# The last chunk of rows finds its 153rd largest value by halving thresholds on ScalarE instead of by repeated MAX8 on VectorE

## The chip, the cores and the metric

One NeuronCore of a Trainium2 chip runs the whole program in one launch. The metric is the device time of an execution in microseconds (us), so lower is better. The kernel before takes 1554.31 us, the median of three runs (1549.61 to 1554.51).

## The reference, cut to what matters

Four residual layers, each followed by a layer norm, over x of 64 x 128 x 512 floats. The change touches layers 0 and 2, which choose neighbours (N = 512 nodes, k = 153):

```python
x_norm = xn / max(norm(xn, axis=-1), 1e-12)
mean_sim = einsum('nbl,mbl->nm', x_norm, x_norm) / B       # 512 x 512
_, idx = top_k(mean_sim, k + 1)                            # per row
# of these the node itself is dropped and the first k = 153 others are kept
mask = zeros((N, N), bool).at[rows, idx].set(keep)
A = where(mask, mean_sim, 0);  deg = A.sum(axis=0)
dinv = where(deg > 0, rsqrt(deg), 0)
An = dinv[:, None] * A * dinv[None, :]
out = einsum('sd,sbl->dbl', An, einsum('nbl,lo->nbo', xn, adj)) + bias
```

So each of the 512 rows needs the set of its 153 largest off-diagonal values, ties going to the lower index, as an exact set: one wrong neighbour changes the result. Layers 1 and 3 (an attention-like pair of kernels, and a plain matmul with a residual weight) are not touched.

## The kernel before, in words

The program is three blocks with a barrier after each: `first_similarity` (sum of x_norm products over all 64 batches, kept in PSUM), then `adjacency` followed by `gnn_layer_pair` (layers 0 and 1, and the similarity sums of layer 2), then `adjacency` followed by `last_layers` (layers 2 and 3). `adjacency` is one function that is called twice; I call the two executions the first and the second choice. Every engine has its own instruction stream in program order, and only semaphores tie the streams together. There is no planner: the order is written out by hand.

In `adjacency`, the 512 rows lie in four chunks of 128 rows (one row per partition, 512 columns). `sim` holds the four chunks, `work` a copy with the diagonal pushed down (`mask`, L532) that the search may destroy. The streams are:

- VectorE (`vector`, L529). `largest(p)` handles a pair of chunks: 19 rounds (`rounds = TOP // 8`), and in each one MAX8 (L545) per chunk, which yields the 8 largest values left, then one MATCH_REPLACE8 (L536) per chunk, which overwrites these 8 in `work` by a marker. TOP % 8 = 1, so a twentieth, shorter round takes one more value (L553 to L558). Then `sim` is multiplied by "work is the marker" (L562), which tells TensorE by the semaphore `chosen`. Pair 0 is done entirely before pair 1. After both, `first_remainders` (L1761, the first choice only) and the degree arithmetic (L589 to L596), and the scaled adjacency in high and low parts (L601, L605).
- TensorE (`tensor`). After the similarity is assembled it computes xw = x * adj for 64 batches, four 128 x 128 x 128 matmuls each, into a ring of four PSUM banks (L624 in the first choice, L679 in the second). In the first choice, 16 jobs that prepare layer 1's weights (L637 to L644) are inserted after batches 16, 19, ..., 61 (`after`). Then it waits for `chosen` of each chunk and adds up the degrees (L692), and spreads dinv over the columns (L698), and only then layer 0 or 2 can start (L1064, L1869).
- ScalarE (`scalar`). It copies each xw out of PSUM (L703, a helper line for every plain copy), to a ring of eight staging tiles in the first choice and to `xres` in the second (a hardware loop there); in the first choice it also takes the prepared weights. Then come `first_roundings` (high parts of the first two xw), a Sqrt of the degrees (L771 loads the table, L773), and the high parts of the adjacency (L703).
- GpSimd (`gpsimd`). In the first choice it computes 12 weight remainders (L788). In the second it has nothing to do between one memset (L779) and `first_remainders` of the next function (L1932).
- SyncE (queue). In the first choice it stores each xw to DRAM (L522), waiting for ScalarE's copy, and for the first 32 batches loads another x after it (L524). In the second it reloads x into a ring of four tiles (L507), each as soon as TensorE has used its tile.

`s.an_hi` and `s.an_lo` (four tiles of 128 x 512 each) are unused until L703 and L605 write them, after the choice.

## Time and profile before

| | before |
|---|---|
| median of 3 runs | 1554.31 us |
| the profiled execution's own time | 1555.39 us |
| its span in the trace | 1553.7 us |
| TensorE busy | 1429.7 us, 92% |
| VectorE busy | 1203.3 us, 77% |
| ScalarE busy | 804.7 us, 52% |
| GpSimd busy | 542.2 us, 35% |
| first choice, first MAX8 to degrees | 148.22 to 256.86 us |
| second choice, first MAX8 to degrees | 1189.32 to 1297.94 us |

How to read it: times are microseconds from the span's start, or ns where marked. Register, branch, semaphore and DMA-issuing instructions aren't counted as busy. "L545" is line 545 of the kernel. "idle before <-releaser" is how long the engine stood still before an instruction, and what ended this. Matmul ends are modelled. An fp32 matmul appears as two or more records.

### The profile page before, as it was taken

How to read it: one execution, taken by the hardware profiler on the slowest of the kernel's cores; microseconds unless marked ns; L12 is line 12 of the kernel's file. 1: busy time of each engine (PE TensorE's matmuls, PEld its weight loads, DVE VectorE, ACT ScalarE, POOL GpSimd, SP SyncE). 2: the span in 40 equal slices, each digit the busy share in tenths (PEclk: the TensorE clock that was granted, in tenths of full speed). 3: DMA queues.
4: the chain of work that ended last, by engine and by line, in shares of the span. 5: the costliest groups of instructions: out<-in, count | busy, mean ns of one | idle time of the engine just before them, and what ended most of it. 6: DMA issues, size and time to landing. Idle time of an engine off the chain costs nothing. (4 is left out here: it accounts for less than half of the span.)

```text
span 1553.7 us, 26749 instructions
## 1 busy us (share of the span) xinstructions
PE 1429.7 (92%) x7544; PEld 1199.4 (77%) x7544; DVE 1203.3 (77%) x3045; ACT 804.7 (52%) x1435; POOL 542.2 (35%) x740
## 2 busy tenths in 40 slices
PE   6998996899999999999999999998998945999996
PEld 5887875688888888888887888877887844777774
DVE  5987997566677766777667776667896996999997
ACT  5754552345434454445545455454553522777775
POOL 5950010112221133223331233322330002999996
PEclk9999997899999999999999999999999976999998
DMA  9803953212221222312232122315603840444443
GB/s 363 286 4 109 404 210 105 66 30 82 74 76 38 81 96 87 101 68 81 74 108 94 62 94 74 125 46 217 217 1 96 242 129 21 137 141 149 142 141 108
DMA packets 88025, 185.60 MB, mean 119 GB/s; under 512 B 9888, under 2 KB 10016, under 8 KB 86432
## 3 DMA queue, kind: packets, MB, share of 16 engines
q1 hardware_dynamic: 87968, 184.92, 34.5%
q8 instruction: 27, 0.44, 0.1%
q14 instruction: 30, 0.25, 0.0%
HBM read 134.55 MB, written 50.33 MB: 119 GB/s over the span
## 5 line engine op out<-in xcount | busy, mean ns | idle before, releaser
L817 POOL TENSOR_TENSOR rs_a<-ve_a,neghalf 128x1 f32<-128x1 f32 x64 | 40.1, 627 | 413.8 <-DVE nm_a L811 413.8
L1110 PE MATMUL bank<-wov,ht_hi 128*128 128x512 f32 x512 | 161.9, 397 | 0.0
L229 PE MATMUL bank<-xn_lo,xn_hi 128*128 128x512 f32 (+1 forms) x640 | 154.5, 373 | 7.6 <-DVE v_lo L1507 4.0
L1507 DVE TENSOR_TENSOR y_lo<-bank,y_hi 128x512 fp32r<-128x512 f32 x128 | 84.1, 687 | 87.3 <-ACT y_hi L1254 87.2
L207 ACT ACTIVATE xn_hi<-xn 128x512 fp32r<-128x512 f32 x128 | 80.8, 631 | 98.0 <-DVE xn L200 74.9
L1932 POOL TENSOR_TENSOR xw_lo<-xres,xw_hi 128x512 fp32r<-128x512 f32 x64 | 82.8, 1295 | 126.0 <-ACT xw_hi L1893 126.0
L212 DVE TENSOR_TENSOR xn_lo<-xn,xn_hi 128x512 fp32r<-128x512 f32 x128 | 116.1, 907 | 9.5 <-ACT xn_hi L207 9.3
L1254 ACT ACTIVATE y_hi<-bank 128x512 fp32r<-128x512 f32 x128 | 70.4, 585 | 101.9 <-PE bank L1083 97.6
L1317 ACT ACTIVATE xo<-xo,nb_b,rs_b 128x512 f32<-128x512 f32 x64 | 52.1, 815 | 132.9 <-POOL nb_b L819 132.9
L220 PEld LDWEIGHTS bank<-xn_hi 128*128 128x128 f32 x512 | 96.7, 193 | 19.4 <-ACT xn_hi L207 1.7
L1083 PE MATMUL bank<-ht_hi,u_lang 128*128 128x512 f32 x320 | 110.8, 395 | 0.8 <-issue 0.7
L1869 PE MATMUL bank<-an_hi,xw_hi 128*128 128x512 f32 x256 | 105.7, 413 | 4.0 <-ACT an_hi L703 2.9
L1083 PE MATMUL bank<-ht_hi,u_grav 128*128 128x512 f32 x320 | 109.2, 390 | 0.0
L1064 PE MATMUL bank<-an_hi,xw_hi 128*128 128x512 f32 x256 | 103.5, 404 | 5.3 <-ACT an_hi L703 2.9
L536 DVE MATCH_REPLACE8 work<-best,work 128x520 f32<-128x520 f32 x160 | 108.2, 683 | 0.0
L229 PEld LDWEIGHTS bank<-xn_lo,xn_hi 128*128 128x128 f32 x640 | 96.0, 195 | 15.4 <-DVE v_lo L1507 4.1
L1110 PEld LDWEIGHTS bank<-wov,ht_hi 128*128 128x128 f32 x512 | 91.8, 189 | 16.1
L1064 PE MATMUL bank<-an_lo,xw_hi 128*128 128x512 f32 x256 | 101.8, 398 | 0.0
L1064 PE MATMUL bank<-an_hi,xw_lo 128*128 128x512 f32 x256 | 101.7, 397 | 0.0
L1869 PE MATMUL bank<-an_hi,xw_lo 128*128 128x512 f32 x256 | 101.7, 397 | 0.0
L1869 PE MATMUL bank<-an_lo,xw_hi 128*128 128x512 f32 x256 | 100.8, 394 | 0.0
L1110 PE MATMUL bank<-wov,ht_lo 128*128 128x512 f32 x256 | 100.2, 391 | 0.0
(225 smaller groups left out, 3978.9 us busy)
## 6 DMA issues: line engine op xcount, KB each, us to landing
xw_dram<-stage SPq DMA_DIRECT2D x64, 256.0 KB, 6.8
stage<-xw_dram SPq DMA_DIRECT2D x64, 256.0 KB, 2.7
stage<-in_x SPq DMA_DIRECT2D x64, 256.0 KB, 2.7
between<-xo SPq DMA_DIRECT2D x64, 256.0 KB, 2.0
xres<-between SPq DMA_DIRECT2D x32, 512.0 KB, 5.9
x_at<-between SPq DMA_DIRECT2D x64, 256.0 KB, 2.9
xin<-between SPq DMA_DIRECT2D x64, 256.0 KB, 2.7
out<-xo SPq DMA_DIRECT2D x64, 256.0 KB, 2.0
```

What stands on the lines that cost most here:

```text
L207: self.nc.scalar.activation(self.hi[:, i % 4, :], self.xn[:, i % 4, :], ACT.Copy).then_inc(self.hi_ready, 1)
L212: self.nc.vector.tensor_tensor(self.lo[:, i % 4, :], self.xn[:, i % 4, :], self.hi[:, i % 4, :].bitcast(F32), ALU.subtract).then_inc(self. ...
L220: self.nc.tensor.matmul(self.at.hh[c], h[:, c * P:(c + 1) * P], h[:, c * P:N], start=(i == 0 and c < 3), stop=False, skip_group_check=True)
L229: mm = self.nc.tensor.matmul(out, h[:, c * P:(c + 1) * P], l[:, a:b], start=(i == 0 and c != 1), stop=False, skip_group_check=True)
L536: nc.vector.match_replace(work[:, c, :], best[:, c, :], work[:, c, :], CHOSEN).then_inc(marked[p], 1)
L1064: mm = nc.tensor.matmul(l0_ps[i % 2][:], xwp[a][:, i % 2, c * P:(c + 1) * P], anp[b][:, c, :], start=(c == 0 and n == 0), stop=(c == CH - ...
L1083: mm = nc.tensor.matmul(yp[k][:], u[a][:, at:at + P], ht[b][:, r, :, :].rearrange("p i n -> p (i n)"), start=(r == 0 and n == 0), stop=(r ...
L1110: mm = nc.tensor.matmul(yp[i % 2][:], ht[a][:, c, i, :], wov[b][:, c, :], start=(c == 0 and n == 0), stop=(c == CH - 1 and n == 2))
L1254: copy = lambda o, i: nc.scalar.activation(o, i, ACT.Copy)
L1507: nc.vector.tensor_tensor(lo, full, hi.bitcast(F32), ALU.subtract).then_inc(done, 1)
L1869: mm = nc.tensor.matmul(l2_ps[i % 2][:], xwp[a][:, i % 2, c * P:(c + 1) * P], anp[b][:, c, :], start=(c == 0 and n == 0), stop=(c == CH - ...
L1932: nc.gpsimd.tensor_tensor(xw_lo[:, i % 2, :], of_batch(ga, i), xw_hi[:, i % 2, :].bitcast(F32), ALU.subtract).then_inc(xw_lo_ok, 1)
```

## The change

Only three chunks (0 to 2, `by_max = 3`) go through MAX8 and MATCH_REPLACE8, all three in each round. Chunk 3 (`late`) is searched by thresholds. ScalarE counts how many values of a row lie above a threshold by Sign with an accumulated sum (one ACTIVATE over 128 x 512 with a pointer bias), and GpSimd turns the count into the next threshold with instructions of 128 x 1. There are 32 counts, one behind every odd batch of the xw loop: one at zero for the sign, 8 leaps over the exponent, 23 halvings over the mantissa. From the fourth batch on they read `lifted`, the rows times plus or minus 2^100. When the last is done, GpSimd derives two neighbouring candidates, and VectorE decides between them, finds the values above and the ties, ranks the ties by a scan, and multiplies `sim`. The ScalarE loop of the second choice is unrolled. The new tiles lie where `an_hi` will be. 24 memsets at the start fill a constant table.

```diff
     def fill(pool):
         nc.gpsimd.memset(s.neghalf[:], -0.5)
+        for k in range(BITS + 1):
+            nc.gpsimd.memset(s.halves[:, k:k + 1], 2.0 ** -min(k + 1, BITS))
...
     def vector(dve):
-        largest(0)
-        dve.wait_ge(copied, 3)
-        mask(2)
-        mask(3)
-        dve.wait_ge(masked, 4)
-        largest(1)
+        eight(0)
+        eight(1)
+        for c in (2, late):
+            dve.wait_ge(copied, c)
+            mask(c)
+        dve.wait_ge(masked, CH)
+        eight(2)
+        for c in range(by_max):
+            dve.wait_ge(found, c + 1)
+            mark(c)
+        with dve.Fori(0, rounds - 1) as r:
+            one_round(r)            # three MAX8, three MATCH_REPLACE8
+        if rest:
+            last_few()
+        dve.wait_ge(lower, CH - 1)
+        reach_high()
+        choose(0)
+        settle()
+        choose(1)
+        above()
+        choose(2)
+        tied()
...
+        def reach_high():
+            dve.wait_ge(kth_near, 5)
+            nc.vector.tensor_scalar(ties[:], row_of(late), high_of[:, 0:1], 0.0, ALU.is_ge, ALU.add,
+                                    accum_out=reached[:, 0:1]).then_inc(ranked, 1)
+        def settle():               # two tensor_scalar of 128 x 1, the second waits for the first
+        def above():
+            dve.wait_ge(ranked, 3)
+            nc.vector.tensor_scalar(signs[:], row_of(late), kth[:, 0:1], 0.0, ALU.is_gt, ALU.add,
+                                    accum_out=reached[:, 1:2]).then_inc(ranked, 1)
+            nc.vector.tensor_scalar(ties[:], row_of(late), kth[:, 0:1], None, ALU.is_equal).then_inc(ranked, 1)
+        def tied():
+            dve.wait_ge(ranked, 5)
+            nc.vector.tensor_scalar(left[:], reached[:, 1:2], -1.0, float(TOP), ALU.mult, ALU.add).then_inc(ranked, 1)
+            nc.vector.tensor_tensor_scan(order_of[:], ties[:], ties[:], 0.0, ALU.add, ALU.max).then_inc(ranked, 1)
+            dve.wait_ge(ranked, 7)
+            nc.vector.scalar_tensor_tensor(out=ties[:], in0=order_of[:], scalar=left[:, 0:1], in1=ties[:],
+                                           op0=ALU.is_le, op1=ALU.mult).then_inc(ranked, 1)
+            dve.wait_ge(ranked, 8)
+            nc.vector.tensor_tensor(signs[:], signs[:], ties[:], ALU.add).then_inc(ranked, 1)
+            dve.wait_ge(ranked, 9)
+            nc.vector.tensor_tensor(sim[:, late, :], sim[:, late, :], signs[:], ALU.mult).then_inc(chosen, 1)
...
     def scalar(act):
+        def count_above(k):
+            act.wait_ge(cut_ready, k + 1)
+            if k == 0:
+                act.wait_ge(masked, CH)
+            nc.scalar.activation(signs[:], row_of(late) if k == 0 else lifted[:], ACT.Sign,
+                                 scale=2.0 ** LIFT if k == 0 else 1.0, bias=cut[:, 0:1],
+                                 accum_out=count_of[:, 0:1]).then_inc(counted, 1)
+        def halve(n):
+            if n % 2:
+                if n == 3:
+                    act.wait_ge(cut_ready, 2)
+                    nc.scalar.activation(lifted[:], row_of(late), ACT.Identity, scale=lift[:, 0:1]).then_inc(lifted_ok, 1)
+                    act.wait_ge(lifted_ok, 1)
+                count_above(n // 2)
                 take_xw(n)
                 if n in after:
                     take_weights(after[n])
+                halve(n)
...
     def gpsimd(pool):
+        def own(instruction):       # issue, then wait for it
+            instruction.then_inc(halved, 1)
+            pool.wait_ge(halved, next(steps))
+        def bit(m):
+            pool.wait_ge(counted, 1 + len(LEAPS) + m)
+            if_reached(step_if, down[:, m - 1:m])        # own(tensor_scalar 128 x 1)
+            scaled(cut, step_if, cut[:, 0:1], up[:, m:m + 1], ALU.add, ALU.add).then_inc(cut_ready, 1)
+        def near_kth():             # three own tensor_scalar, two side by side, one more that waits for these
+        for n in range(nb):
+            if weights is not None and n in after:
+                weight_remainder(after[n])
+            if n == 1:
+                sign_found()        # six own tensor_scalar and a memset
+            elif n % 2 and n // 2 <= len(LEAPS):
+                leap(n // 2 - 1)    # two tensor_scalar, the last leap five
+            elif n % 2:
+                bit(n // 2 - len(LEAPS))
+        near_kth()
```

## Rows read from the trace of the kernel before

**Rows 1.** Waits, whole span: engine and line waited for, us in total, times, longest.

```profile
PE bank L692 <- DVE sim L562: 41.3, 2, 32.2
```

**Rows 2.** Timeline around the end of the second choice: start us, us, engine, line, operation.

```profile
1260.57 0.60 ACT L703 ACTIVATE xres<-bank 128x512 f32 x1 [0.74 <-PE bank L679]
1261.91 2.50 POOL L1932 TENSOR_TENSOR xw_lo<-xres,xw_hi 128x512 fp32r<-128x512 f32 x2 [80.00 <-ACT xw_hi L1893]
...
1290.78 1.29 DVE L553 MAX8 best<-work 128x8 f32<-128x520 f32 x2
...
1293.59 1.28 DVE L562 SCALAR_TENSOR_TENSOR sim<-work,sim 128x512 f32<-128x512 f32 x2
...
1294.33 3.57 PE L692 MATMUL bank<-ones_r,sim 128*128 128x1 f32 x16 [32.20 <-DVE sim L562]
1297.94 0.16 DVE L589 TENSOR_SCALAR deg<-bank 128x4 f32<-128x4 f32 x1 [3.06 <-PE bank L692]
```

**Rows 3.** Timeline around the start of the second choice.

```profile
1189.32 1.30 DVE L545 MAX8 best<-work 128x8 f32<-128x520 f32 x2 [0.44 <-DVEq L540]
...
1190.15 1.15 ACT L703 ACTIVATE work<-sim 128x512 f32<-128x512 f32 x2
...
1191.43 0.60 ACT L703 ACTIVATE xres<-bank 128x512 f32 x1
1191.87 1.29 DVE L545 MAX8 best<-work 128x8 f32<-128x520 f32 x2
```

**Rows 4.** Timeline around the end of the first choice.

```profile
240.68 0.60 ACT L703 ACTIVATE tmp<-bank 128x512 f32<-128x512 f32 x1 [2.84 <-PE bank L640]
...
241.85 1.22 ACT L703 ACTIVATE stage<-bank 128x512 f32<-128x512 f32 x2
242.02 1.27 POOL L788 TENSOR_TENSOR wov<-tmp,wov 128x512 fp32r<-128x512 f32 x1 [4.83 <-ACT wov L703]
242.27 1.84 PE L692 MATMUL bank<-ones_r,sim 128*128 128x1 f32 x16
...
252.51 1.28 DVE L562 SCALAR_TENSOR_TENSOR sim<-work,sim 128x512 f32<-128x512 f32 x2
...
253.25 3.57 PE L692 MATMUL bank<-ones_r,sim 128*128 128x1 f32 x16 [9.14 <-DVE sim L562]
...
256.86 0.16 DVE L589 TENSOR_SCALAR deg<-bank 128x4 f32<-128x4 f32 x1 [1.86 <-PE bank L692]
```

**Rows 5.** Windows: the two halves of the first xw loop, then the second xw loop.

```profile
149.06:189.56 40.50, 39.57 (x296) 35.00 (x297) 40.50 (x97) 24.02 (x44) 1.28 (x1) 1.00 1.05 395
189.56:243.10 53.54, 53.54 (x339) 42.52 (x337) 53.02 (x127) 28.91 (x57) 10.57 (x11) 1.00 0.54 204
1190.00:1261.20 71.20, 65.50 (x521) 61.23 (x522) 70.68 (x169) 39.38 (x68) 0.00 (x0) 1.00 0.77 234
```

**Rows 6.** Groups by form: line, engine, operation, shapes, count | busy us, mean ns | idle before.

```profile
L1309 ACT ACTIVATE a_g<-a_g,inv_s 128x512 f32<-128x512 f32 x16 | 11.6, 724 | 29.4 <-DVE a_g L1574 29.4
L771 ACT ACTIVATE warm<-warm 128x1 f32<-128x1 f32 x2 | 0.4, 194 | 0.0
L819 POOL TENSOR_TENSOR nb_a<-nm_a,rs_a 128x1 f32<-128x1 f32 x64 | 12.1, 190 | 5.0
L817 POOL TENSOR_TENSOR rs_a<-ve_a,neghalf 128x1 f32<-128x1 f32 x64 | 40.1, 627 | 413.8 <-DVE nm_a L811 413.8
L1497 POOL TENSOR_TENSOR r_l<-q_l,neghalf 128x4 f32<-128x4 f32 x16 | 16.4, 1026 | 33.5 <-DVE q_l L1551 33.5
L1574 DVE TENSOR_SCALAR a_g<-a_g 128x512 f32<-128x512 f32 x16 | 6.8, 427 | 0.6
L596 DVE TENSOR_SCALAR dcol<-dinv 128x4 f32<-128x4 f32 x2 | 0.3, 170 | 0.1
L771 ACT ACT_TABLE_LOAD x1 | 1.3, 1283 | 0.0
```

**Rows 7.** Timeline, GpSimd, start of the span.

```profile
14.19 1.27 POOL L273 TENSOR_TENSOR acc<-sq 128x512 f32<-128x512 f32 x1 [11.08 <-ACT sq L372]
```

More of the change, by code:

```diff
@@ L24 @@
 NEVER = -2.0 ** 126
+BELOW_ALL = -2.0 ** 20
+LIFT, FLOOR = 100, -50
+LEAPS = [79, 40, 20, 10, 5, 3, 2, 1]
+BITS = 23
 CHOSEN = -2.0 ** 127
@@ L459, in adjacency @@
     an_hi, an_lo = s.an_hi, s.an_lo
+    by_max, late = CH - 1, CH - 1
+    lifted, signs = s.place("lifted", s.an_at, (N,)), s.place("signs", s.an_at + 1, (N,))
+    ties, order_of = s.place("ties", s.an_at + 2, (N,)), s.place("order_of", s.an_at + 3, (N,))
+    count_of, cut, base, step_if = (sb(n, [P, 1]) for n in ("count_of", "cut", "base", "step_if"))
+    lift, back, passes_at = (sb(n, [P, 1]) for n in ("lift", "back", "passes_at"))
+    down, up = sb("down", [P, BITS + 1]), sb("up", [P, BITS + 1])
+    one_of, two_of, low_of, high_of, gap_of = (sb(n, [P, 1]) for n in ("one_of", "two_of", "low_of", "high_of", "gap_of"))
+    reached, kth, left = sb("reached", [P, 2]), sb("kth", [P, 1]), sb("left", [P, 1])
+    counted, cut_ready, halved, lifted_ok = (sem(x) for x in ("counted", "cut_ready", "halved", "lifted_ok"))
+    kth_near, ranked = sem("kth_near"), sem("ranked")
     at = Layout(banks[:6])
@@ new lines, in eight, with mark, one_round @@
+        def eight(c):
+            nc.vector.max(best[:, c, :], work[:, c, :]).then_inc(found, 1)
+        def mark(c):
+            nc.vector.match_replace(work[:, c, :], best[:, c, :], work[:, c, :], CHOSEN).then_inc(marked, 1)
+        def one_round(r):
+            for c in range(by_max):
+                dve.wait_ge(marked, by_max * r + c + 1)
+                own_step(dve, passed)
+                eight(c)
+            for c in range(by_max):
+                dve.wait_ge(found, by_max * r + by_max + c + 1)
+                own_step(dve, passed)
+                mark(c)
@@ new lines, in last_few, with choose @@
+        def last_few():
+            for c in range(by_max):
+                dve.wait_ge(marked, by_max * (rounds - 1) + c + 1)
+                eight(c)
+            dve.wait_ge(found, by_max * (rounds + 1))
+            nc.vector.memset(best[:, 0:by_max, rest:8], NEVER).then_inc(found, 1)
+            dve.wait_ge(found, by_max * (rounds + 1) + 1)
+            for c in range(by_max):
+                mark(c)
+        def choose(c):
+            dve.wait_ge(marked, by_max * (rounds - (0 if rest else 1)) + c + 1)
+            nc.vector.scalar_tensor_tensor(out=sim[:, c, :], in0=row_of(c), scalar=CHOSEN, in1=sim[:, c, :],
+                                           op0=ALU.is_equal, op1=ALU.mult).then_inc(chosen, 1)
@@ L757, in scalar @@
                     take_weights(after[n])
+                halve(n)
         else:
-            def batch(b):
-                return xres[:, bass.ds(b, 1), :].rearrange("p a n -> p (a n)")
-            def take(b, k):
-                act.wait_ge(xw_made, b + 1)
-                copy(batch(b), xw_ps[k][:]).then_inc(xw_out, 1)
-            with act.Fori(0, nb // 4) as q:
-                for k in range(4):
-                    take(4 * q + k, k)
+            for n in range(nb):
+                act.wait_ge(xw_made, n + 1)
+                copy(xres[:, n, :], xw_ps[n % 4][:]).then_inc(xw_out, 1)
+                halve(n)
         engines.following.first_roundings(act)
@@ L778, in gpsimd @@
     def gpsimd(pool):
-        nc.gpsimd.memset(warm[:], 1.0).then_inc(warmed, 1)
-        if weights is not None:
-            k = 0
-            for kind, name, c in jobs:
-                if kind == "turn":
-                    continue
-                w = N - c * P if name != "ov" else N
-                d = [x[:, c, :] if name == "ov" else x[:, TRI[c]:TRI[c] + w] for x in dst[name]]
-                pool.wait_ge(w_hi, k + 1)
-                nc.gpsimd.tensor_tensor(d[1], tmp[:, k % 2, 0:w], d[0].bitcast(F32),
-                                        ALU.subtract).then_inc(w_lo, 1)
-                k += 1
+        steps = count(1)
@@ new lines, in weight_remainder @@
+        def weight_remainder(n):
+            kind, name, c = jobs[n]
+            if kind == "turn":
+                return
+            k = n - CH
+            w = N - c * P if name != "ov" else N
+            d = [x[:, c, :] if name == "ov" else x[:, TRI[c]:TRI[c] + w] for x in dst[name]]
+            pool.wait_ge(w_hi, k + 1)
+            nc.gpsimd.tensor_tensor(d[1], tmp[:, k % 2, 0:w], d[0].bitcast(F32), ALU.subtract).then_inc(w_lo, 1)
+        nc.gpsimd.memset(warm[:], 1.0).then_inc(warmed, 1)
```

76 lines of the change are left out of this document (46 added, 30 removed).

## Prediction

> **What bounds the kernel now.** I read the waits first. TensorE, 92% busy over the whole span, stands still for 41.3 us behind one line: L692, the degrees, waits for L562, the choice on VectorE; it does so twice, and one of the two waits is 32.2 us [rows 1]. The timeline shows them. In the second choice ScalarE has taken its last xw at 1261.17, but the last choice ends at 1293.59 + 1.28 = 1294.87, and the degrees are there at 1297.94 [rows 2]. In the first choice the xw loop ends at 243.07, the choice at 253.79, the degrees at 256.86, after a wait of 9.1 us [rows 4]. So VectorE sets the end of both choices, but its lead over the xw loop is 33.7 us in the second and only 10.7 us in the first. This lead is the most that a shorter search can give, and the change also adds work to the loop and a tail behind it. The windows tell what room the loop has: ScalarE is busy 24.0 of 40.5 us, 28.9 of 53.5 us and 39.4 of 71.2 us, GpSimd 1.3, 10.6 and 0 us [rows 5]. TensorE fills the middle window (53.5 of 53.5), the first runs at 395 GB/s.
>
> **Part 1, VectorE loses one chunk.** Two chunks take 1191.87 - 1189.32 = 2.55 us a round [rows 3], 1.27 us a chunk. Twenty rounds of it are 25.4 us, which go from each choice. Now the new end of the search. First round of the second choice: two MAX8 end at about 1190.6, but row copies 2 and 3 are ready on ScalarE only at 1190.15 + 1.15 = 1191.3 [rows 3]; the mask of chunk 3 takes 0.3 us more, the third MAX8 and three replacements are done at about 1194.2. 18 rounds of 3 x 1.27 us are 68.6, to 1262.8. The last round took 1293.59 - 1290.78 = 2.81 us for two chunks [rows 2], so 4.1 for three: 1266.9. In the first choice everything is 41.1 us after 148.2 as well, so VectorE is free at 225.8.
>
> **Part 2, 32 counts on ScalarE.** No ACTIVATE with an accumulated sum is in the trace. Its body: 0.72 us, by L1309, which has a pointer operand too [rows 6]; back to back two ACTIVATEs overlap by 0.1 us (two of 0.63 in 1.15, [rows 3]). For fetching the sum I take a small instruction, 0.19 us as L771 [rows 6]. Together c = 0.82 us. Bounds: 0.62 (sum free) to 1.34 (the sum costs another pass of 0.72). In the second choice a pair of batches takes (1260.57 - 1191.43) / 63 x 2 = 2.19 us [rows 2, 3]; ScalarE needs 0.60 + 0.60 + 0.82 = 2.02 of it, so it fits, barely, and a delay of a copy is soaked up by four PSUM banks. The last count follows the copy that ended at 1261.17, ends at 1262.0, and with a lag of 1 us at 1263.0. In the first choice the weight jobs matter: in the last group ScalarE starts on weights at 240.68 and on the next copies at 241.85, GpSimd subtracts from 242.02 to 243.29 [rows 4], and only then steps the threshold (0.5 us, part 3), so count 31 runs from 243.9 to 244.7. Earlier groups don't pile up: ScalarE has 28.9 + 16 x 0.82 = 42.0 us of work in 53.5, and in the first window 24.0 + 16 x 0.82 = 37.1 in 40.5 [rows 5]. The sign step at n = 1 (seven GpSimd instructions) and the lifted copy (0.6 us) delay the start by 1 to 2 us, before either loop is pressed by ScalarE.
>
> **Part 3, GpSimd between the counts.** Nearest row: L819, 128 x 1, 0.19 us, and 0.07 us to the next by semaphore: p = 0.26 us a step. Bounds: nothing, and 1.10 (L1497, a power on 128 x 4, 1.03); L817, a power on 128 x 1, gives 0.70 [rows 6]. I take 0.26, since these are multiplications, comparisons and sums as L819 is. Two steps, 0.5 us, fit beside the two copies of 1.2 us. Behind the last count: two steps of the bit and six of `near_kth`, 8 x 0.26 = 2.1 us. So the candidates are ready at 1265.1 in the second choice (VectorE comes at 1266.9: hidden, with 1.8 us of room) and at 246.8 in the first (VectorE has waited since 225.8: exposed).
>
> **Part 4, the tail on VectorE.** Two-input passes over 128 x 512: 0.64 us each by L562 (1.28 for two, [rows 2]); with a wait on the one before, 0.74. The pass with one input and no sum: 0.43 us by L1574; small ones 0.2 by L596 [rows 6]. In order: `reach_high` 0.7, choose 0.64, `settle` 0.4, choose 0.64, `above` 0.7 + 0.43, choose 0.64, left 0.15, scan, then three dependent passes 3 x 0.74 = 2.2. Without the scan this is 6.5. No scan is in the trace: bounds 0.64 as any pass, and 2.0 as three such passes. I take twice 0.6, 1.2, since each element needs the sum before it. Tail: 7.7 us, bounds 6.7 (with the sums free) and 9. The Trainium skill (DVE: opcode table, instruction layouts, handler registers and perf-mode slots; Datapath and trigger behaviour) says that the built-in scan runs at half throughput because its feedback goes through an earlier stage. No row here shows a scan; by that page it is 1.2 us, by the plain pass 0.6, which is 0.5 us in each choice.
>
> **Part 5, TensorE behind the last choice.** Before, chunks 2 and 3 came together: 16 records in 3.57 us, degrees 3.07 us after the last choice [rows 2, 4]. Now only chunk 3 is left by then, 8 records, 1.8 us, so the degrees come 1.9 us after it. The two `first_remainders` in the first choice (1.3 us, between `tied` and the degrees on VectorE) stay under these 1.9.
>
> **Part 6, at no cost.** 24 memsets at the start, at most the 0.19 us of L819 each [rows 6], 4.6 us, stand where GpSimd idles 11.1 us before its first sum [rows 7]; without that cover they cost as much. The Sqrt table load, 1.28 us [rows 6], sits behind the loop in both choices, under the tail; it would be late only if the tail went. GpSimd's xw remainders of the second choice (2.50 us, [rows 2]) now stand behind `near_kth`, at 1265.1 to 1267.6, needed at about 1282. VectorE waiting in `reach_high` holds up chooses 0 to 2, but TensorE needs all four chunks anyway.
>
> **Sum.** Second choice: 1266.9 + 7.7 + 1.9 = 1276.5 against 1297.94: -21.4. First choice: 246.8 + 7.7 + 1.9 = 256.4 against 256.86: -0.5. Of 50.8 us taken from VectorE 21.9 are left, since the first choice is now held by the loop, the relay and the tail. What is late next is the relay in the first, still VectorE in the second. 1555.39 - 21.9 = 1533.5 against the profiled execution; the median is 1.08 lower, which gives 1532.4. I say 1533. Its own range, from the tail (-2 to +2.6), a last count earlier or later by 1 in the first choice, and the spread of the runs, is 1529 to 1538.
>
> **Rivals.**
> - *The relay sets the loop (GpSimd's steps are dear).* From one count to the next: c + 0.1 + 2p. For: POOL's small powers take 0.63 to 1.03. Against: L819 beside them takes 0.19 [rows 6]. At p = 0.70 the relay is 2.3 us against 2.19: the last count ends at 1192.9 + 31 x 2.3 + 0.9 = 1265.1, plus 8 x 0.70 = 5.6 gives 1270.7, 3.8 us after VectorE is free; in the first choice GpSimd's last bit is 0.9 later and the eight steps 3.5 longer, so +3.9 less 0.5. Total -21.4 + 3.8 - 0.5 + 4.4 = -13.7, **1541**.
> - *The other side: the same relay at p above 0.95.* Then both loops run at 0.9 + 2p. Second choice, degrees at 1192.9 + 31 (0.9 + 2p) + 0.9 + 8p + 7.7 + 1.9; first choice the same from 151.7. Against 1297.94 and 256.86 the sum is zero at p = 0.97, and each further 0.1 us costs 14 us. At p = 1.10, L1497's price, it's 1554.3 + 18 = **1572**. A dearer form of it: if Sign and Copy needed different tables, each count would carry two loads of 1.28 us. Against: L771's load is the only one in either choice (x1, [rows 6]), though the copies of L703 follow an Exp in the first and a Sqrt in the second. The Trainium skill (ScalarE: Activation LUTs; Table sets) says that cheap functions such as copy and identity are in every set; it doesn't name Sign for each, and a single load is absorbed.
> - *The sum on ScalarE costs a second pass, c = 1.34.* For: on VectorE such a sum is read by an extra instruction. Against: there it is short. A pair then needs 2.54 us: the second loop ends at 1191.4 + 32 x 2.54 = 1272.7, candidates 1274.8, degrees 1284.4, -13.5; in the first, about 3 us of stalls and a longer last count, +3. Total -10.5, **1544**. It decides from c = 1.0 on.
> - *TensorE's clock doesn't fall.* L692's 16 records take 1.84 us right behind the loop at 242.27 and 3.57 us after standing for 9.1 us [rows 4]: 2.4 and 1.2 GHz. The waits that are left are of the same kind, so I expect the low clock again; if it stayed high, the eight last records save 0.9 us, and what follows them at the low clock (an estimate by the same ratio, over some 4 us) 2 us more, 3 us a choice: **1527**.
>
> **How the numbers follow.** Chances: the forecast 0.66, dear relay 0.13, sum as a pass 0.10, clock 0.04, the other side (relay over 0.97 or tables) 0.06, something that cancels the gain 0.01. The range 1529 to 1542 holds the first and second and the near half of the third. About 0.3% (4.7 us) is what a measurement of this kernel tells from no change. Faster by more than that: 0.66 + 0.13 + 0.10 + 0.04 = 0.93, less 0.01 for the edges, 0.92; within it 0.02; slower 0.06.
>
> **What would show it.** Right: VectorE goes from the last replacement to `reach_high` without standing in the second choice, and stands some 21 us in the first; counts every 2.2 us with two copies between; ScalarE's wait for GpSimd near zero; the last xw copy of the second loop before 1263; `chosen` 3 at about 1274.6 and 254.5; the wait of L692 down to under 14 us in the second. Wrong: a pair of batches over 2.3 us in the second loop, small GpSimd instructions over 0.4 us, a tail over 9 us, or a table load in each pair.

## The result, and the profile after

The kernel after takes 1534.26 us (median of 4 executions, 1532.57 to 1536.30), the kernel before beside it 1552.67 us: a ratio of 0.9877, 95% interval 0.9859 to 0.9894, 18.4 us faster. A second comparison gave 1534.30 against 1554.53, 0.9875 [0.9853, 0.9896], 20.2 us. The forecast was 1533, in a range of 1529 to 1542.

The table cuts the span of every profiled execution at the same marks. A choice runs from its first MAX8 to its degrees (the operation `deg<-bank`); what lies ahead of it, from ScalarE's first `stage<-bank` on, is the assembly of the similarity. "Middle" is everything from the first degrees to the second assembly; no line of the change runs there.

| us | start | assembly | choice 1 | middle | assembly | choice 2 | end | span |
|---|---|---|---|---|---|---|---|---|
| before | 142.07 | 6.15 | 108.64 | 924.97 | 7.49 | 108.62 | 255.76 | 1553.7 |
| after | 140.91 | 7.38 | 108.70 | 922.10 | 7.24 | 87.80 | 256.67 | 1530.8 |
| after, again | 142.62 | 5.74 | 110.27 | 921.48 | 5.75 | 87.44 | 255.40 | 1528.7 |
| only_second | 140.80 | 7.73 | 108.62 | 920.89 | 5.75 | 88.30 | 256.01 | 1528.1 |
| only_first | 141.37 | 7.38 | 109.88 | 924.91 | 7.56 | 108.62 | 255.88 | 1555.6 |
| slow_relay | 141.18 | 5.75 | 114.61 | 920.87 | 5.74 | 99.54 | 255.41 | 1543.1 |
| count_twice | 142.18 | 7.27 | 115.46 | 921.27 | 5.75 | 95.80 | 256.27 | 1544.0 |
| no_tie_rank | 142.98 | 5.74 | 109.54 | 925.16 | 8.36 | 86.48 | 256.54 | 1534.8 |
| early_counts | 140.94 | 7.29 | 112.07 | 921.35 | 5.74 | 88.15 | 256.56 | 1532.1 |
| early_reordered | 141.46 | 5.75 | 111.16 | 920.85 | 5.74 | 87.89 | 256.75 | 1529.6 |
| chooses_first | 140.72 | 7.27 | 108.38 | 921.51 | 5.75 | 87.80 | 256.77 | 1528.2 |
| chooses_first_no_rank | 141.23 | 7.31 | 103.63 | 921.64 | 5.74 | 86.88 | 255.67 | 1522.1 |
| early_kth | 141.60 | 5.74 | 102.17 | 925.41 | 7.04 | 88.15 | 256.39 | 1526.5 |
| early_kth_reordered | 142.74 | 5.75 | 98.20 | 925.80 | 7.14 | 88.92 | 256.05 | 1524.6 |

Between the first two rows the second choice lost 20.8 us and the first lost nothing (+0.06). The rest of the 22.9 us between the spans, 2.1 us, lies in parts that hold no line of the change, above all the middle (-2.9). The middle comes at 921 to 922 or at about 925 us, whatever the kernel, so I read experiments by the choices and use the medians as a second witness. Each row is one execution: the two of the kernel after differ by 1.6 us in choice 1, because its xw loop ended 94.5 us after the first MAX8 in one and 96.1 us in the other.

The traces show what the levels of the middle are. All five executions at 925 have a stretch of TensorE at the low clock that the nine others don't have, some 155 us ahead of the second assembly. The same work in before and in only_second (window, length, PE, PEld, DVE, ACT, POOL busy with counts, granted clock, DMA share, GB/s):

```profile
1024.50:1029.50 5.00, 5.00 (x21) 4.25 (x22) 3.09 (x5) 1.69 (x4) 0.00 (x0) 0.66 0.00 0
1023.40:1028.40 5.00, 4.97 (x28) 4.38 (x29) 3.09 (x5) 2.35 (x5) 0.00 (x0) 1.00 0.00 0
```

Ahead of both TensorE had stood for the same 1.47 us; a granted clock of 0.5 is 1.2 GHz here and 1.00 is 2.4 GHz. In these traces this stretch and a longer low one some 40 us later make 2.7 us of the difference. The assembly goes the same way: 5.7 to 6.2 us in all executions where its clock was 1.00, 7.0 to 7.7 us where it was 0.76, 8.4 us where it was 0.54. What decides which executions get the low stretch is open.

The waits of the kernel after, over the whole span, as in [rows 1]:

```profile
PE bank L757 <- DVE sim L581: 15.1, 2, 7.7
DVE ties L586 <- POOL gap_of L862: 21.2, 1, 21.2
```

TensorE waited 41.3 us for VectorE's choices, now 15.1 and, for the last multiplication (L612), 0.79 us twice. VectorE in turn stands 21.2 us, once, for the candidates that GpSimd hands over. The timeline says where. The second choice of the kernel after, which answers to [rows 2, 3] (start us, us, engine, line, operation, then the idle time before and what ended it):

```profile
1186.33 1.30 DVE L554 MAX8 best<-work 128x8 f32<-128x520 f32 x2
...
1188.75 0.60 ACT L768 ACTIVATE xres<-bank 128x512 f32<-128x512 f32 x1
...
1258.50 0.60 ACT L768 ACTIVATE xres<-bank 128x512 f32<-128x512 f32 x1 [0.51 <-PE bank L744]
1258.99 0.71 ACT L802 ACTIVATE signs<-lifted,cut 128x512 f32<-128x512 f32 x1
1259.60 0.19 ACT L802 ACTIVATION_READ_ACCUMULATOR signs<-lifted,cut 128x1 f32 x1
1259.69 1.14 ACT L2028 ACTIVATE xw_hi<-xres 128x512 fp32r<-128x512 f32 x2
1259.89 0.37 POOL L865 TENSOR_SCALAR step_if<-count_of,passes_at,down 128x1 f32<-128x1 f32 x1 [1.44 <-ACT signs L802]
...
1262.81 0.29 POOL L862 TENSOR_SCALAR gap_of<-high_of,low_of 128x1 f32<-128x1 f32 x1 [0.17 <-POOL high_of L862]
1263.06 2.49 POOL L2067 TENSOR_TENSOR xw_lo<-xres,xw_hi 128x512 fp32r<-128x512 f32 x2
1264.38 0.73 DVE L586 TENSOR_SCALAR_CACHE_REDUCE ties<-work,high_of 128x512 f32<-128x512 f32 x1
1265.04 1.06 DVE L581 SCALAR_TENSOR_TENSOR sim<-work,sim 128x512 f32<-128x512 f32 x1
...
1266.15 5.28 PE L757 MATMUL bank<-ones_r,sim 128*128 128x1 f32 x24 [7.70 <-DVE sim L581]
1266.39 0.68 DVE L581 SCALAR_TENSOR_TENSOR sim<-work,sim 128x512 f32<-128x512 f32 x1
...
1268.72 1.21 DVE L605 TENSOR_TENSOR_SCAN order_of<-ties 128x512 f32<-128x512 f32 x1
...
1271.48 0.69 DVE L612 TENSOR_TENSOR sim<-sim,signs 128x512 f32<-128x512 f32 x1
1272.22 1.87 PE L757 MATMUL bank<-ones_r,sim 128*128 128x1 f32 x8 [0.79 <-DVE sim L612]
1274.13 0.16 DVE L654 TENSOR_SCALAR deg<-bank 128x4 f32<-128x4 f32 x1 [1.96 <-PE bank L757]
```

VectorE goes on to `reach_high` (L586) at 1264.38 with no wait in front, because `gap_of` had ended at 1263.10: the relay is hidden, by 1.3 us. Behind that the tail of one chunk runs 7.8 us. The first choice, answering to [rows 4]:

```profile
241.21 1.27 POOL L912 TENSOR_TENSOR wov<-tmp,wov 128x512 fp32r<-128x512 f32 x1 [4.00 <-ACT wov L768]
...
241.74 1.06 ACT L768 ACTIVATE stage<-bank 128x512 f32<-128x512 f32 x2
...
243.35 0.72 ACT L802 ACTIVATE signs<-lifted,cut 128x512 f32<-128x512 f32 x1 [0.55 <-POOL cut L862]
...
244.26 0.37 POOL L865 TENSOR_SCALAR step_if<-count_of,passes_at,down 128x1 f32<-128x1 f32 x1 [0.94 <-ACT signs L802]
...
247.17 0.29 POOL L862 TENSOR_SCALAR gap_of<-high_of,low_of 128x1 f32<-128x1 f32 x1 [0.17 <-POOL high_of L862]
247.60 0.75 DVE L586 TENSOR_SCALAR_CACHE_REDUCE ties<-work,high_of 128x512 f32<-128x512 f32 x1 [21.16 <-POOL gap_of L862]
...
249.01 5.28 PE L757 MATMUL bank<-ones_r,sim 128*128 128x1 f32 x24 [7.40 <-DVE sim L581]
...
255.09 1.87 PE L757 MATMUL bank<-ones_r,sim 128*128 128x1 f32 x8 [0.79 <-DVE sim L612]
...
256.99 0.16 DVE L654 TENSOR_SCALAR deg<-bank 128x4 f32<-128x4 f32 x1 [0.76 <-PE bank L757]
```

Here the last weight remainder (L912) ends at 242.48, just ahead of the loop's end at 242.80. Only then does GpSimd form the last threshold, so the last count (L802) comes after the loop, and VectorE, free since 247.60 - 21.16 = 226.4, waits for what follows from it. Both timelines show in the same way something I had missed: the sums of chunks 0 to 2 (24 records) take 5.28 us from the first choose on (a choose is the multiplication of `sim` for one chunk), and end 0.79 us before those of chunk 3 can start. Tail and sums cover the same stretch: shortening one alone leaves the other.

The windows of the loops after (from to, length, PE, PEld, DVE, ACT, POOL busy with counts, granted clock, DMA share, GB/s), for [rows 5]:

```profile
149.50:188.00 38.50, 37.68 (x290) 33.94 (x291) 37.64 (x92) 32.82 (x72) 12.86 (x39) 1.00 1.05 394
188.00:242.80 54.80, 53.62 (x337) 42.39 (x335) 38.33 (x92) 39.06 (x91) 22.32 (x42) 1.00 0.54 205
1188.75:1259.10 70.35, 63.68 (x504) 58.70 (x502) 70.31 (x168) 58.11 (x128) 23.63 (x70) 1.00 0.78 236
```

ScalarE rose from 39.4 to 58.1 us of busy time in the second loop and the loop got hardly longer: 70.35 us from the first copy to the end of the last, 69.74 before [rows 2, 3].

### The profile page after: what moved, and what is told of

Read it like the earlier page. It is cut to its first block and busy times, and to the rows that moved or that the text cites. A ratio compares the mean times of both kernels' runs of the same rounds, so it can differ in the third digit from the quotient of the medians.

```text
span 1530.8 us, 26694 instructions
## 1 busy us (share of the span) xinstructions
PE 1431.6 (94%) x7544; PEld 1201.5 (78%) x7544; DVE 1162.9 (76%) x2945; ACT 844.9 (55%) x1565; POOL 595.2 (39%) x922
## 5 line engine op out<-in xcount | busy, mean ns | idle before, releaser
L952 POOL TENSOR_TENSOR rs_b<-ve_b,neghalf 128x1 f32<-128x1 f32 x64 | 34.8, 543 | 179.2 <-DVE nm_b L946 179.2
L1245 PE MATMUL bank<-wov,ht_lo 128*128 128x512 f32 x256 | 100.1, 391 | 0.0
L227 PE MATMUL bank<-xn_hi 128*128 128x512 f32 (+3 forms) x512 | 97.3, 313 | 1.6 <-ACT xn_hi L214 1.4
```

The source lines that it names most:

```text
L227: self.nc.tensor.matmul(self.at.hh[c], h[:, c * P:(c + 1) * P], h[:, c * P:N], start=(i == 0 and c < 3), stop=False, skip_group_check=True)
L952: nc.gpsimd.tensor_tensor(root, var_eps, neghalf, ALU.pow).then_inc(root_ok, 1)
L1245: mm = nc.tensor.matmul(yp[i % 2][:], ht[a][:, c, i, :], wov[b][:, c, :], start=(c == 0 and n == 0), stop=(c == CH - 1 and n == 2))
```

## The experiments

Each kernel is the kernel after with the edit shown ("..." marks lines left out); its line numbers shift by the lines of the edit. Medians go with that of the kernel before on the same chip (1555.22 for the first four, 1554.53 for the next four, 1554.77 for the last four).

**Which choice carries the gain (only_second, only_first).** The adjacency function of the kernel before is added as `adjacency_max` and called in one place; the mirror image is the same edit in the other call.

```diff
-            adj_1 = adjacency(nc, s, sb, sem, banks, weights, None, (xr, x, xw_dram, first_loads))
+            adj_1 = adjacency_max(nc, s, sb, sem, banks, weights, None, (xr, x, xw_dram, first_loads))
```

> The new search runs in the second choice only; the first choice is that of the kernel before. Theory (the whole gain is the chunk that VectorE no longer searches in the second choice, where it set the end; the first choice gives nothing because its end is set by the loop, the last count and the exposed tail): second choice from first MAX8 to degrees 87.8 us as in the changed kernel (108.6 before), first 108.6; time 20 to 21 us below the kernel before, equal to the changed kernel within 2 us. Rival (both choices share the gain, or the layers between run faster by about 3 us because of the change, as the two profiles would have it: 924.97 us before and 922.10 us after from the first degrees to the second block): only about half to three quarters of the gain, 10 to 17 us.

> The new search runs in the first choice only. Theory: no change of time that can be told (within 2 us of the kernel before); first choice 108.7 us from first MAX8 to degrees, second 108.6. Rival (shared gain): 5 to 10 us below the kernel before. Other side: the counts lengthen the first loop, 3 us above.

only_second 1530.24 us, ratio 0.985 [0.9826, 0.9873], choice 2 88.30 us. only_first 1556.60 us, 1.0006 [0.9992, 1.0020], choice 1 109.88 us. So the second choice has all of it, and the first gives nothing or costs about 1 us. The -25 us of only_second is more than its choice explains (-20.3) and more than I had expected; its middle is 4.1 us shorter than that of before in the profiled execution, the lower of the two levels above. Four of its five executions have a mean granted clock of 0.974 or 0.975 and take 1527.4 to 1530.5 us, the fifth has 0.970 and takes 1534.8, as the kernel after does at 0.970. I claim only the 20.3.

**How near is the relay (slow_relay).** Two idle steps of 128 x 1 on GpSimd in each leap and bit.

```diff
+            for _ in range(2):
+                own(nc.gpsimd.tensor_scalar(idle_of[:], passes_at[:, 0:1], passes_at[:, 0:1], 1.0, ALU.is_ge, ALU.mult))
```

> As the changed kernel, with two idle GpSimd instructions (128 x 1, each awaited, about 0.4 us) in every threshold step, so that count to count takes at least about 2.5 us instead of 1.7, against 2.19 us for a pair of batches. Theory (the relay is just below the pace of the second loop, and VectorE is only 1.3 us later than the candidates): the second choice is now set by the relay: last count about 79 us after the first, candidates about 88 us after the first MAX8 instead of 76.8, so about 10 us longer; the first choice, whose loop is 20 us longer, gets 1 us at most. Total about 11 us above the changed kernel, still below the kernel before. Rival (GpSimd is hidden anyway in both): less than 3 us above the changed kernel.

1548.28 us, 0.9969 [0.9955, 0.9983], 14 us above the kernel after (11 forecast); choice 2 99.54 us, +11.7. Now the counts come every 2.56 us and each waits for GpSimd; the last line is count 31 of the first choice:

```profile
1226.22 0.72 ACT L803 ACTIVATE signs<-lifted,cut 128x512 f32<-128x512 f32 x1 [0.78 <-POOL cut L863]
...
1228.78 0.72 ACT L803 ACTIVATE signs<-lifted,cut 128x512 f32<-128x512 f32 x1 [0.78 <-POOL cut L863]
...
247.14 0.72 ACT L803 ACTIVATE signs<-lifted,cut 128x512 f32<-128x512 f32 x1 [1.32 <-POOL cut L863]
```

The mechanism of the second choice is as forecast. The first choice lost 5.9 us against after (4.3 against its other execution), where I had said at most 1. A relay of 2.56 us leaves no room in a pair of the first window (40.5 us for 32 batches [rows 5], 2.53 a pair), and in the second window each weight remainder (1.27 us on GpSimd) stands inside the relay: the loop ended 98.9 us after the first MAX8 instead of 94.5 or 96.1. The candidates came 6.2 us behind the loop's end instead of 4.7, since four idle steps stand behind it. A pair has more time here than in the second choice (2.2 us), but what the relay loses behind the loop nothing covers.

**What a dearer count costs (count_twice).** A second summed ACTIVATE over the same tile ahead of each count, without a bias and without a semaphore of its own.

```diff
+            nc.scalar.activation(order_of[:], row_of(late) if k == 0 else lifted[:], ACT.Sign,
+                                 scale=2.0 ** LIFT if k == 0 else 1.0, accum_out=again_of[:, 0:1])
```

> As the changed kernel, with a second Sign pass with a sum (without bias, result unused) in front of each count: 0.7 us more of ScalarE for each pair of batches, 0.7 us more in the relay too. Theory (ScalarE has 0.2 to 0.3 us of room in a pair in the second loop and little more in the first half of the first): a pair in the second loop takes 2.55 to 2.6 us, candidates 8 to 10 us after VectorE is free; first choice 3 to 7 us longer. Total 12 to 16 us above the changed kernel. Rival (the loops are held by the loads and TensorE, ScalarE is hidden): less than 3 us above it.

1544.71 us, 0.9943 [0.9921, 0.9966]; choice 2 95.80 (+8.0), choice 1 115.46 (+6.8). That is 10.5 us above the kernel after, less than the 12 to 16 that I had expected. A pair is now 2.42 us, not 2.55 to 2.6:

```profile
1267.65 0.63 ACT L803 ACTIVATE order_of<-lifted 128x512 f32<-128x512 f32 x1
...
1270.07 0.63 ACT L803 ACTIVATE order_of<-lifted 128x512 f32<-128x512 f32 x1
```

ScalarE needs 0.60 + 0.60 + 0.70 = 1.9 of the 2.2 us of a pair in the kernel after, so it is 0.3 us from setting the second loop; past that, each 0.1 us in a count costs 32 times as much, 3.2 us in that choice. The rival "the sum is a second pass" is excluded in the kernel itself by the durations of L802, 0.71 and 0.19.

**The kernel after again, and the tail alone (after_again, no_tie_rank).** no_tie_rank leaves out the rank of ties: all values at or above the 153rd are taken, so scan and three passes go.

```diff
-            nc.vector.tensor_scalar(signs[:], row_of(late), kth[:, 0:1], 0.0, ALU.is_gt, ALU.add,
+            nc.vector.tensor_scalar(signs[:], row_of(late), kth[:, 0:1], 0.0, ALU.is_ge, ALU.add,
...
-            nc.vector.tensor_tensor_scan(order_of[:], ties[:], ties[:], 0.0, ALU.add, ALU.max).then_inc(ranked, 1)
...
-            nc.vector.tensor_tensor(signs[:], signs[:], ties[:], ALU.add).then_inc(ranked, 1)
```

> The changed kernel once more, as the base for the three kernels beside it: 20 us below the kernel before in the median (18 to 23), first MAX8 to degrees 108.7 us in the first choice and 87.8 us in the second.

> As the changed kernel without the ranking of ties: the late chunk takes every value from its 153rd on, with no equality pass, scan, comparison and sum. Theory (VectorE's tail is exposed in full in both choices): 0.40 + 0.07 + 1.25 + 0.79 + 0.73 = 3.2 us less in each, 105.5 and 84.6 us from first MAX8 to degrees, 6.4 us in all. Rival (in the first choice the Sqrt table and the xw remainders are as late, so the tail is only partly exposed there): 3 to 4 us in all.

after_again 1534.30, no_tie_rank 1534.23 us, 0.9862 [0.9843, 0.9881]. after_again came as expected in its time, but its first choice took 110.27 us and not 108.7, for the loop's end named above. So a first choice is best counted from the end of `gap_of`, the last step of the candidates: from there to the degrees it takes 9.53 us in both executions of the kernel after, and 8.57 in no_tie_rank. The second choice is 1.0 us shorter than in after_again. Both give 1.0 us, not the 3.2 I had expected, nor nothing. The first choice of no_tie_rank shows why:

```profile
251.23 6.99 PE L748 MATMUL bank<-ones_r,sim 128*128 128x1 f32 x32 [7.43 <-DVE sim L581]
...
253.34 0.68 DVE L603 TENSOR_TENSOR sim<-sim,signs 128x512 f32<-128x512 f32 x1
258.26 0.16 DVE L645 TENSOR_SCALAR deg<-bank 128x4 f32<-128x4 f32 x1 [3.03 <-PE bank L748]
```

VectorE is done at 254.02, but TensorE sums all 32 records without a pause, 6.99 us from the first choose on. They run at 0.22 us a record behind the wait of 7.4 us; the 16 right behind the loop in [rows 4] took 0.115 each. What the tail gives up, the sums take.

**Sums out of the tail's way (chooses_first, chooses_first_no_rank).** The three choices that don't need the candidates go ahead of the wait for them; the second kernel also leaves the rank of ties out.

```diff
+        for c in range(by_max):
+            choose(c)
         reach_high()
-        choose(0)
         settle()
-        choose(1)
         above()
-        choose(2)
```

> As the changed kernel, but VectorE multiplies sim for chunks 0 to 2 before it waits for the candidates of the late chunk. Theory (in the changed kernel the degree sums on TensorE, 24 records in 5.3 us from the first choose on, run only 0.8 us ahead of the last one, so they and the tail end together; both are released by the candidates in the first choice): first choice, the three chooses leave the tail and TensorE has done their sums before: 1.9 us shorter; second choice, where nothing was released early, the same within 0.5 us. Total 1 to 2 us, which the times will hardly tell. Rival (the order of the passes does not matter): both choices the same within 0.5 us.

> chooses_first without the ranking of ties (the late chunk takes every value from its 153rd on). Theory (leaving the ranking out alone gave 1.1 us or less a choice instead of 3.2 because TensorE's sums of chunks 0 to 2 took its place): in the first choice these sums are done, so now the whole 3.2 us show, 5 us shorter than the changed kernel; in the second they start with the first choose as before and end as before, so 1 to 1.5 us shorter than the changed kernel. Rival (the ranking is cheap in itself): the first choice as in chooses_first within 1 us.

1531.68 us, 0.9862 [0.9846, 0.9879], and 1526.00 us, 0.9823 [0.9804, 0.9843]. In the first choice of chooses_first the 24 records run right behind the loop, at the high clock:

```profile
242.34 2.74 PE L756 MATMUL bank<-ones_r,sim 128*128 128x1 f32 x24
...
254.46 1.87 PE L756 MATMUL bank<-ones_r,sim 128*128 128x1 f32 x8 [9.39 <-DVE sim L612]
```

Alone that moves choice 1 by -0.3 us against after and -1.9 against after_again, which by itself doesn't tell my expectation (-1.9) from its rival (within 0.5). From the end of `gap_of` to the degrees it is 7.99 us instead of 9.53 in either, so the order is worth 1.5 us. Choice 2 is as in after (87.80), since there VectorE doesn't wait and the order makes no difference. With the rank gone as well, choice 1 falls to 103.63, and the stretch behind `gap_of` to 4.76: 4.8 us less, against 1.0 for the rank alone and 1.5 for the order alone. In choice 2 the same kernel gives 0.9 us, of 1 to 1.5 forecast. The two together give nearly twice their sum: each was the other's cover, as the failed expectation of no_tie_rank suggested.

**Counts that end before the loop (early_counts, early_reordered).** In the first choice the counts stand on two batches of three, so the last is at batch 47 and not 63. early_reordered also moves ScalarE's first roundings behind the Sqrt table load and VectorE's first remainders behind the degrees.

```diff
+    slots = [n for n in range(nb) if n % 3][:1 + len(LEAPS) + BITS] if weights is not None else [*range(1, nb, 2)]
-            if n % 2:
+            if n in slots:
```

> As the changed kernel, but in the first choice the 32 counts stand behind two of three batches instead of every second, so the last is behind batch 47 at about 213 us. Theory (the first choice is held by the last count and what follows it): VectorE goes into its tail at 226 and is done at 234, before the loop ends; then the xw high parts (248 to 249.1), the Sqrt table (to 250.4) and the xw remainders hold the degrees, at 250 instead of 257: 6 to 7 us below the changed kernel. Rival (counts closer together than the relay lengthen the loop by 3 us or more, since ScalarE stands for GpSimd): gain below 3 us, or none.

> As early_counts, and in the first choice ScalarE takes the Sqrt table and the root before the first high parts of xw, and VectorE the degrees before their remainders. Theory: the degrees follow the loop directly, at about 246.5, the scaled adjacency some 5 us later, after the xw parts at 250 to 251; layer 0 starts about 10 us earlier than in the changed kernel, 3.5 to 4 us below early_counts. Rival (the xw parts, whose loads wait for the last stores, hold layer 0): no gain over early_counts.

1531.88 us, 0.9852 [0.9835, 0.9868], and 1531.84 us, 0.9857 [0.9839, 0.9874]. Both expectations failed: choice 1 is 112.07 and 111.16 us, longer than in either execution of after. Lines of early_counts:

```profile
171.00 0.72 ACT L803 ACTIVATE signs<-lifted,cut 128x512 f32<-128x512 f32 x1 [1.50 <-POOL cut L864]
...
247.25 1.26 POOL L914 TENSOR_TENSOR wov<-tmp,wov 128x512 fp32r<-128x512 f32 x1 [4.84 <-ACT wov L769]
248.50 0.31 POOL L864 TENSOR_SCALAR cut<-cut 128x1 f32<-128x1 f32 x1
...
250.91 0.75 DVE L587 TENSOR_SCALAR_CACHE_REDUCE ties<-work,high_of 128x512 f32<-128x512 f32 x1 [24.55 <-POOL gap_of L864]
```

There are two reasons. The steps that form the candidates stayed behind the last weight remainder in GpSimd's order: they start at 248.50, at its end, though the last count was long past. And where two counts stand a single copy apart, ScalarE waits 0.3 to 0.5 us for GpSimd, and once 1.5 us, and has more counts to do: the sixteenth xw copy ends 24.1 us after the first MAX8 instead of 18.4 or 19.6, and the loop 100.1 us after it instead of 94.5 or 96.1. That the medians are still 2.4 us under after_again is within the spread of the middle; I draw nothing from it.

**Both mended (early_kth, early_kth_reordered).** Counts on odd batches up to 31, then two of three up to 55; each count ahead of the weights; the candidates right behind the last count; the three choices first. The second kernel adds early_reordered's moves.

```diff
+        slots = [n for n in range(nb) if (n % 2 if n < 32 else n % 3 != 0)][:1 + len(LEAPS) + BITS]
...
+            if k == len(LEAPS) + BITS:
+                near_kth()
...
-        near_kth()
```

> chooses_first, and in the first choice 16 counts behind every second batch up to batch 31, then 16 behind two of three up to batch 55, each ahead of the weights of its batch, and GpSimd derives the candidates right behind the last count, not behind all weight remainders. Theory (the first choice is held by the last count; the closer counts of early_counts lengthened its loop in the first half, where ScalarE has no room, and its candidates still stood behind the last weight remainder): the loop ends as in the changed kernel within 1 us, VectorE is done before it, and the xw parts and the Sqrt table hold the degrees at about 102 us after the first MAX8 instead of 108.7 to 110.3: layer 0 starts 6 to 7 us earlier. Rival (the counts lengthen the loop again by 5 us): 2 us at most.

> early_kth, and in the first choice ScalarE takes the Sqrt table and the root before the first high parts of xw, VectorE the degrees before their remainders. Theory: degrees about 98.5 us after the first MAX8, layer 0 at about 104.5 instead of 114.6 to 116.2: 10 to 11 us below the changed kernel, 1522 to 1525 us. Rival (the xw parts, whose loads wait for the last stores, hold layer 0): no gain over early_kth.

early_kth 1528.26 us, 0.9819 [0.9801, 0.9836], choice 1 102.17; its degrees wait for `first_remainders` on VectorE, which end at 249.6 behind the load of the stored xw. **early_kth_reordered 1523.80 us (1520.83 to 1526.30), 0.9798 [0.9785, 0.9812]**, choice 1 98.20, the lowest median of all and 31.0 us under before. The numbers of both expectations held. Its first choice:

```profile
231.54 0.75 DVE L589 TENSOR_SCALAR_CACHE_REDUCE ties<-work,high_of 128x512 f32<-128x512 f32 x1 [3.11 <-POOL gap_of L868]
...
236.85 1.64 DVE L615 TENSOR_TENSOR sim<-sim,signs 128x512 f32<-128x512 f32 x1
...
243.02 3.63 PE L759 MATMUL bank<-ones_r,sim 128*128 128x1 f32 x32
246.69 0.16 DVE L655 TENSOR_SCALAR deg<-bank 128x4 f32<-128x4 f32 x1 [8.19 <-PE bank L759]
```

VectorE waits 3.1 us instead of 21.2 and has chosen everything at 238.5, before the loop ends; TensorE sums 32 records in 3.63 us straight behind it, and the degrees are there. Layer 0's first product starts 104.9 us after the first MAX8, 114.6 in after and in before. The time that the change takes from VectorE in the first choice could be had all along; what held it back was where the search by counts ends, and what stands behind it in each engine's order.

## Why the prediction was right

The sum was -21.9 us: -21.4 in the second choice, -0.5 in the first. The traces show -20.8 and +0.06 (+1.2 to +1.6 in two other executions), the medians -18.4 and -20.2. The mechanism is the one that was forecast; that the first choice came so near is in part the luck of that execution, whose loop ended early. The price list of the small operations in the first choice of the kernel after (line, engine, operation, shapes, count | busy us, mean ns | idle before):

```profile
L862 POOL TENSOR_SCALAR cut<-step_if,cut,up 128x1 f32<-128x1 f32 x23 | 8.7, 378 | 2.3
L865 POOL TENSOR_SCALAR step_if<-count_of,passes_at 128x1 f32<-128x1 f32 x8 | 2.4, 297 | 10.1 <-ACT signs L802 10.1
L872 POOL TENSOR_SCALAR one_of<-count_of 128x1 f32<-128x1 f32 x3 | 0.7, 231 | 12.1 <-ACT signs L802 12.0
```

- **Part 1 held.** VectorE is free 78.05 us after the first MAX8 in the second choice (77.6 worked out) and waits 21.2 us in the first ("some 21"). only_second and only_first show that the whole gain is in the choice with the long lead. (The first choice lies 1041.1 us ahead of the second, where that part has "41.1 us"; its 225.8 = 148.2 + 77.6 isn't touched by it.)
- **Part 2 held, its price too high.** c is 0.70, not 0.82: the next instruction starts 0.70 us after the count (1258.99 to 1259.69), beside the reading of the sum. A pair takes 70.35 / 32 = 2.2 us, as forecast. count_twice shows that the room was 0.3 us wide. No table load came with Sign.
- **Part 3, a size off.** A step costs 0.23 us with constants, 0.30 with one pointer and 0.38 with two; with its wait up to 0.48, against p = 0.26. The last eight take 3.2 us (244.26 to 247.46), not 2.1. Hidden in the second choice (room 1.3 us instead of 1.8), exposed in the first, where the candidates came 0.6 us later than worked out, which is the miss of the first choice in this execution. That the earlier counts cost the loop nothing isn't shown: it ended 93.5 and 94.8 us after the first MAX8 in two executions without counts (only_second, before), and 94.2 to 96.3 in the six with the counts on every odd batch and no other load (after, after_again, only_first, no_tie_rank and the two chooses_first), so it may cost 1 us. slow_relay shows the next bound: its two idle steps made 2.56 us of a relay of 1.8, and a pair has 2.2, so 0.4 us more would be enough.
- **Part 4 held.** The tail is 7.4 us in the first and 7.8 in the second, 7.7 forecast. The scan takes 1.21 us, against 0.69 for L612 on the same tile. By the Trainium skill's rule on the scan's feedback (DVE: opcode table, instruction layouts, handler registers and perf-mode slots; Datapath and trigger behaviour) it was to be 1.2; the trace agrees.
- **Part 5 right in its number, wrong in its reason.** The degrees come 1.96 us after the last choice (1.9 forecast). But the sentence that waiting in `reach_high` costs nothing, "TensorE needs all four chunks anyway", failed: the 24 earlier sums need 5.28 us at the low clock and end just ahead of the tail, by 0.79 us. A shorter tail would have been worth a fraction of its size (no_tie_rank: 1.0 of 3.2 us in each), and the order costs 1.5 us in the first choice, more as the tail shrinks (chooses_first_no_rank: 4.8 us for both).
- **Part 6 held, with two slips.** The 24 memsets take 0.86 us together, under an idle time of 10.0 us. The xw remainders stood behind `near_kth` as said, but not free: they can collide with a choose (0.38 us here, 0.87 in only_second, nothing in after_again; below). The Sqrt table is loaded behind the loop in the first choice only (249.14); the second has no load.
- **The rivals.** Relay and count could both have set the loop, and do so when made dearer (slow_relay 1548, count_twice 1545). TensorE's clock stayed low behind the wait that was left, as it had been before (granted 0.50 over both groups of sums, 249.01 to 254.29 and 1266.15 to 1271.43). In the rival "the other side" the formulas as written cross zero at p = 0.95, not 0.97, and give 1575 at p = 1.10, not 1572; neither touches the range.

Not settled: why the low clock comes in the middle of some executions and not of others. Before and only_first are at 925 us, and so are no_tie_rank and both early_kth, which hold the change in both choices, so it isn't that; no run was aimed at it.

## What to carry to other kernels

A unit of work taken from the engine that ends last is worth at most its lead over what runs beside it, and the lead differs between two uses of the same code: read both ends in the timeline (33.7 us and 10.7 here) before costing the edit. When a serial search is spread over a loop as count, step, count, its last link counts most: end it some iterations early and put what hangs on it ahead of other jobs in that engine's order; here that was worth 6.0 us against after_again (early_kth, which also has the chooses first), and 10.5 with the table load and the degrees ahead of the xw parts (early_kth_reordered), half of the change itself. If an experiment that removes a visible cost gives a fraction of it, look for a second piece of work over the same stretch and remove both. When one execution stands for a kernel, count from the event that the edit acts behind, so that the spread ahead of it drops out.

## What the runs showed of the hardware

**VectorE and GpSimd hold each other up.** In these traces passes with two inputs from SBUF ran over their usual time beside a GpSimd operation that had started first, and the other way round. In the kernel after, the choose at 1265.04 took 1.06 us instead of 0.68 beside GpSimd's `xw_lo`, and ended 0.55 us after it (1265.55). In early_kth_reordered the multiplication at 236.85 took 1.64 us instead of 0.69: it ended 0.55 us after GpSimd's subtraction (237.94), the third line below; and a step of 128 x 1 took 1.17 us instead of 0.38 beside three chooses. In chooses_first VectorE was first, by 0.04 us: its three chooses kept their time, and `xw_lo` took 2.97 us instead of 1.27 (the last two lines):

```profile
226.54 1.88 DVE L584 SCALAR_TENSOR_TENSOR sim<-work,sim 128x512 f32<-128x512 f32 x3
...
227.51 1.17 POOL L871 TENSOR_SCALAR step_if<-count_of,passes_at,down 128x1 f32<-128x1 f32 x1 [0.95 <-ACT signs L804]
...
236.66 1.28 POOL L918 TENSOR_TENSOR wov<-tmp,wov 128x512 fp32r<-128x512 f32 x1 [3.92 <-ACT wov L770]
...
1261.68 1.89 DVE L581 SCALAR_TENSOR_TENSOR sim<-work,sim 128x512 f32<-128x512 f32 x3
1261.72 2.97 POOL L2066 TENSOR_TENSOR xw_lo<-xres,xw_hi 128x512 fp32r<-128x512 f32 x1
```

The pass with one input, `reach_high` at 1264.38, kept its time beside the same `xw_lo` (0.73 us, 0.75 with GpSimd idle). This collision is the spread of choice 2: 87.44 us with none (after_again), 87.80 with a choose of 1.06 us (after), 88.30 with one of 1.55 us (only_second).

The Trainium skill (SBUF — State Buffer; Who interferes with whom, and SBUF: two separate sides) describes the port pair that the two engines share as an exclusive lock: the later one is blocked until the earlier one's instruction ends. The cases on VectorE fit that, and so does the direction in chooses_first. Both GpSimd operations outlasted more than one choose, though, the small step by 0.25 us after the third had ended, so the order within a row of chooses isn't settled. No experiment was aimed at it.

**A summed ACTIVATE is cheap for its engine, less so for its reader.** The sum costs ScalarE some 0.09 us of a 128 x 512 tile: in count_twice the summed pass without a pointer starts at 1267.65 and the next instruction at 1268.28, 0.63 us later, while behind a plain pass of the same 0.63 us (`wov<-tmp` of the kernel after, 240.50) the next starts after 0.53 to 0.54. With the pointer it is 0.70. GpSimd's first step starts 0.90 us after the count's start (1258.99 to 1259.89).

**TensorE's sums tell the clock.** A record of 128 x 1 takes 0.115 us right behind the loop (granted clock 1.00 over 242.34 to 245.08 of chooses_first) and 0.22 us after 7 us of standing (0.50 over 249.01 to 254.29 of the kernel after), 2.4 and 1.2 GHz, so 24 of them cost 2.74 or 5.28 us depending on when the data come.
